# One transformer tower on one core: preparing steps, order of the maxima, place of three weight pieces, and the gates' small tiles in PSUM

## The reference, cut to what matters

```python
h = W.T[x] + b + positions                      # embedding
h = h + attn(layernorm(h))                      # 8 heads of 16, linear scores, normalised per row
y = softmax(causal(l2norm(q) * l2norm(k))) @ v @ Wo      # 2 heads of 64, on layernorm(h) twice
gate = softmax(y @ gate_W + gate_b)             # over E = 8 experts
hid  = gelu(y @ W1[e] + b1[e])                  # FF = 512 per expert
out  = sum_e gate[e] * (hid @ W2[e] + b2[e])
h = h + out
```

## Time and profile before

| | us |
|---|---|
| profiled execution, device time | 850.87 |
| its span | 849.1 |
| median of three runs | 852.5 |
| PE busy | 777.6 |
| DVE busy | 710.1 |
| ACT busy | 478.3 |
| POOL busy | 341.3 |

### The profile page before, as it was taken

The page is one execution under the profiler, slowest core; times in us unless marked ns, Lnnn a source line. Parts: engine busy times, 40 slices in busy tenths (PEclk is TensorE's granted clock), DMA queues, the critical chain, the costliest instruction groups (busy, mean ns, idle before and its releaser), DMA issues.

```text
span 849.1 us, 21002 instructions
## 1 busy us (share of the span) xinstructions
PE 777.6 (92%) x8208; PEld 555.6 (65%) x8208; DVE 710.1 (84%) x1585; ACT 478.3 (56%) x997; POOL 341.3 (40%) x386
## 2 busy tenths in 40 slices
PE   2799999999876789998889889999999999999997
PEld 1668887788644455555556556777777777777775
DVE  3668899888489776776777878999999999999997
ACT  2436555555255667776879666455555555555553
POOL 6649999777365557666667530000000000000000
PEclk9899999999799999999999999999999999999999
DMA  3101011000000000000000000000000000000000
GB/s 130 56 8 35 23 38 38 25 26 17 10 1 1 1 2 2 2 3 2 2 14 3 2 2 2 2 14 2 14 1 14 2 14 2 14 2 14 2 14 14
DMA packets 9666, 12.09 MB, mean 14 GB/s; under 512 B 1856, under 2 KB 6592, under 8 KB 9568
## 3 DMA queue, kind: packets, MB, share of 16 engines
q1 hardware_dynamic: 8544, 8.65, 3.4%
q0 software_dynamic: 1024, 2.10, 0.9%
HBM read 8.65 MB, written 2.10 MB: 13 GB/s over the span
## 4 chain that ended last, share of the span: by engine, by line
PE 75%; DVE 9%; ACT 7%; issue 5%; POOL 2%; DMA 1%; DVEq 0%; ACTq 0%; POOLq 0%
PE ps L988 73%; DVE mx L834 2%; DVE room L944 1%; ACT room L562 1%; DVE room L942 1%; ACT room L553 1%; ACT qk L492 1%; DMA h_all<-emb_rows,idx 1%; DVE mx L829 1%; PE ps L1016 1%; DVE och L911 0%; ACT qh L499 0%; PE ps L996 0%; ACT kh L501 0%; ACT hxT L481 0%
## 5 line engine op out<-in xcount | busy, mean ns | idle before, releaser
L577 ACT ACTIVATE cst<-ps,col 128x512 f32<-128x512 f32 x256 | 176.1, 689 | 164.0 <-PE ps L988 163.2
L988 PEld LDWEIGHTS ps<-arena,sq 128*128 128x128 f16 x3072 | 192.2, 98 | 62.1 <-DVE sq L972 4.2
L988 PE MATMUL ps<-arena,sq 128*128 128x128 f16 x3072 | 213.1, 219 | 0.5 <-DVE sq L972 0.5
L988 PE MATMUL ps<-y,arena 128*128 128x512 f16 x768 | 208.7, 382 | 1.3 <-DVE och L911 1.3
L972 DVE TENSOR_TENSOR sq<-cst,sq 128x512 f16<-128x512 f32 x256 | 175.8, 687 | 4.4
L373 POOL TENSOR_TENSOR room<-room 128x512 f16<-128x512 f32 (+3 forms) x122 | 123.6, 1032 | 74.2 <-ACT room L562 72.6
L967 DVE CAST sq<-cst 128x512 f16<-128x512 f32 x256 | 108.9, 425 | 11.5 <-ACT cst L577 4.2
L553 ACT ACTIVATE room<-ps 128x512 f32<-128x512 f32 (+3 forms) x160 | 76.7, 533 | 41.3 <-PE ps L988 40.9
L834 DVE TENSOR_REDUCE mx<-ps 128x2 f32<-128x1024 f32 (+2 forms) x64 | 70.1, 1096 | 30.4 <-PE ps L988 30.2
L988 PEld LDWEIGHTS ps<-y,arena 128*128 128x128 f16 x768 | 65.0, 98 | 34.0 <-issue 3.4
L960 DVE SCALAR_TENSOR_TENSOR h_all<-ps,gs,h_all 128x128 f32<-128x128 f32 x256 | 77.2, 344 | 1.0 <-PE ps L988 0.9
(11 more groups left out here) (158 smaller groups left out, 1186.9 us busy)
## 6 DMA issues: line engine op xcount, KB each, us to landing
sq<-w_rows SPq DMA_DIRECT2D x16, 256.0 KB, 2.8
out<-h_all SPq DMA_DIRECT2D x32, 64.0 KB, 1.6
cst<-consts SPq DMA_DIRECT2D x1, 896.0 KB, 5.3
h_all<-emb_rows,idx POOLq DMA_INDIRECT x32, 2.6
cst<-consts SPq DMA_DIRECT2D x1, 398.0 KB, 3.3
c<-consts SPq DMA_DIRECT2D x1, 256.0 KB, 5.1
wqkv<-w_qkv SPq DMA_DIRECT2D x1, 192.0 KB, 3.4
wsm<-w_sm SPq DMA_DIRECT2D x1, 192.0 KB, 5.1
```

Of the source, the lines that this page charges most:

```text
L577: a.activation(hid[:, f], ps[:, HBANK[f], :], ACT.Gelu_apprx_tanh, bias=col[:, K_B1 + k:K_B1 + k + 1], scale=1.0 / WS).then_inc(S["hid_rea ...
L988: return t_.matmul(o, l, r, start=start, stop=stop, skip_group_check=True)
```

## The change

The second norm from block 3 on is applied by ScalarE, with a scale and a bias that POOL and VectorE prepare; its transposition moves to the head of the preparing step. The small constant of the l2 norm is put into a 65th column of the squares, so that one addition on POOL goes. In attention the last piece of each step's pair_scores moves behind values and output parts. The three late weight pieces are treated in expert steps 2, 7 and 13, from staging tiles of their own, and the gates' biased logits and exponentials lie in bank 5 instead of in SBUF; the next user of bank 5 waits for the finished gates. In `normed_T` and `out_T` some wait counts move by one with the order.

```diff
-        eps = sb("eps", [P, 10])
-        ln_eps, l2_eps = eps[:, 0:2], eps[:, 2:10]
+        ln_eps = sb("eps", [P, 2])[:]
-        rr = sb("rr", [P, NT, 2, B])
+        rr = sb("rr", [P, NT, 4, B])
-        qk2 = sb("qk2", [P, B, 4 * DS])
+        qk2 = sb("qk2", [P, B * 4, DS + 1])
-        gt = sb("gt", [P, 2, 4, E])
+        gt = sb("gt", [P, 4, E])
+        biased = ps[:, 5, 4 * E:8 * E].rearrange("p (r e) -> p r e", e=E)
+        raised = ps[:, 5, 8 * E:12 * E].rearrange("p (r e) -> p r e", e=E)
+        late_stage = [x2_all[:].rearrange(...), hxT_all[:].rearrange(...)]
...
 SyncE
-            for n in range(2, NPIECE):
+            for n in range(2, NEARLY):
                 ...
+            sp.wait_ge(S["qkv2_ps"], NT)
+            sp.wait_ge(S["x2T_ps"], NT)
+            for n in range(NEARLY, NPIECE):
+                sp.wait_ge(S["wlow_ready"], n - 1)
+                sp.dma_start(late_stage[n % 2], w12_rows[...]).then_inc(S[STAGED[n % 2]], 16)
...
 GpSimd, both_norms
-                g.tensor_tensor(rr[:, c, 1], rr[:, c, 0], mhalf[:, 0:B], ALU.pow).then_inc(S["rr_ready"], 1)
+                g.tensor_tensor(rr[:, c, 1], rr[:, c, 0], mhalf[:, 0:B], ALU.pow).then_inc(S["neg2"], 1)
+                pool.wait_ge(S["neg2"], c + 1)
+                g.tensor_tensor(rr[:, c, 3], rr[:, c, 1], rr[:, c, 2], ALU.mult).then_inc(S["rr_ready"], 1)
 GpSimd, l2_factors
-                g.tensor_tensor(ss[:, par, 1], ss[:, par, 0], l2_eps, ALU.add).then_inc(S["l2_link"], 1)
-                pool.wait_ge(S["l2_link"], c + 1)
-                g.tensor_tensor(ss[:, par, 2], ss[:, par, 1], mhalf[:, 0:8], ALU.pow).then_inc(S["rn_ready"], 1)
+                g.tensor_tensor(ss[:, par, 1], ss[:, par, 0], mhalf[:, 0:8], ALU.pow).then_inc(S["rn_ready"], 1)
 GpSimd, end of attention
-                if s in WLATE:
-                    weights_low(NEARLY + WLATE.index(s))
+            weights_low(NEARLY)
+            weights_low(NEARLY + 1)
             low_y(LAST)
+            weights_low(NEARLY + 2)
...
 ScalarE
+            def normed2(c):
+                act.wait_ge(S["rr_ready"], c + 1)
+                act.wait_ge(S["x2T_ps"], c - 1)
+                for b in range(B):
+                    last = a.activation(x2[c % 2][:, b], h_all[:, 2 * c + b, :], ACT.Identity,
+                                        bias=rr[:, c, 3, b:b + 1], scale=rr[:, c, 1, b:b + 1])
+                last.then_inc(S["x2_ready"], 1)
             def step_b(c):
+                if c and c + 3 < NT:
+                    normed_T(c + 3)
                 if c + 2 < NT:
                     squares(c + 2)
                 high_qk(c)
                 if c == 4:
                     ao_out(NT - 1)
-                if c + 3 < NT:
-                    normed_T(c + 3)
+                if c == 0:
+                    normed_T(3)
+                if c + 4 < NT:
+                    normed2(c + 4)
+            normed2(3)
 ...
-                    a.activation(gt[:, 1], gt[:, 0], ACT.Exp).then_inc(S["eg_ready"], 1)
+                    a.activation(raised, gt[:], ACT.Exp).then_inc(S["eg_ready"], 1)
 ... (attention loop)
-                    if s in WLATE:
-                        weights_high(NEARLY + WLATE.index(s))
 ... (expert loop)
+                    if n * FT + f in WLATE:
+                        weights_high(NEARLY + WLATE.index(n * FT + f))
...
 VectorE, stats2
+                v.tensor_scalar(rr[:, c, 2], mv2[:, c, :, 0], -1.0, None, ALU.mult).then_inc(S["stats2"], 1)
 VectorE, step_b
-                if c + 3 < NT:
-                    normed2(c + 3)
 VectorE, out_part (gt[:, 0] and gt[:, 1] become)
+                    v.tensor_tensor(biased, lg, row[...], ALU.add)
+                    v.tensor_reduce(gl[:, 0], biased, AX, ALU.max)
+                    v.tensor_tensor(gt[:], biased, gl[:, 0]..., ALU.subtract)
+                    v.tensor_reduce(gl[:, 1], raised, AX, ALU.add)
+                    v.scalar_tensor_tensor(gs[:, m], raised, 1.0 / WS, gl[:, 2]..., ALU.mult, ALU.mult)
...
 TensorE, step_b
+                if c and c + 3 < NT:
+                    normed_T(c + 3)
                 if c + 2 < NT:
                     pe.wait_ge(S["qkn_ready"], c + 1)
                     project2(c + 2)
                 ...
                 unit_T(c)
-                if c + 3 < NT:
-                    normed_T(c + 3)
+                if c == 0:
+                    normed_T(3)
 TensorE, out_part 3
-                    bank5 = S["lg_ready"], m + 1
+                    bank5 = S["gate_ready"], m + 1
 TensorE, attention loop
-                for part in pairs[:1]:
+                for part in pairs[:-1]:
                     pair_scores(*part)
                 ... values(s - LAG, 0), values(s - LAG, 1) ...
-                for part in pairs[1:]:
-                    pair_scores(*part)
                 for m in range(LAST):
                     if s - YAT[m] in PE_Y:
                         out_part(m, PE_Y.index(s - YAT[m]) + 1)
+                for part in pairs[-1:]:
+                    pair_scores(*part)
 TensorE, down (experts)
+                    if NEARLY - E <= n < E:
+                        pe.wait_ge(S["wlow_ready"], E + n + 1)
-WLATE = [52, 60, 66]
+WLATE = [2, 7, 13]
```

More of the change, by code:

```diff
@@ L50, in sem @@
             return ctx.enter_context(nc.semaphore(name))
+        ps = ctx.enter_context(nc.psum_tensor("ps", [P, 8, 512], F32))
         cst = sb("cst", [P, C_END])
@@ L304, in _ @@
             g.memset(mpad[:], 0.0).then_inc(S["setup"], 1)
[L305 removed]
+            pool.wait_ge(S["setup"], 9)
             pool.wait_ge(S["load_a"], 32)
@@ L345, in _ @@
                 weights_low(n)
+            g.memset(qk2[:, :, DS:], L2_EPS).then_inc(S["eps_set"], 1)
             out_bias(NT - 1)
@@ L430, in weights_high @@
                 act.wait_ge(S[STAGED[n % 2]], 16 * (n // 2 + 1))
-                a.activation(w12[:, 4 * n:4 * n + 4, 0, :], stage[n % 2].rearrange("p (w d) -> p w d", d=D),
+                raw = stage[n % 2] if n < NEARLY else late_stage[n % 2]
+                a.activation(w12[:, 4 * n:4 * n + 4, 0, :], raw.rearrange("p (w d) -> p w d", d=D),
                              ACT.Copy, scale=WS)
-                a.activation(scaled[n % 2], stage[n % 2], ACT.Copy, scale=WS).then_inc(S["whigh_ready"], 1)
+                a.activation(scaled[n % 2], raw, ACT.Copy, scale=WS).then_inc(S["whigh_ready"], 1)
             a.preload_act_table(ACT.Exp)
@@ L491, in squares @@
                     act.wait_ge(S["wlow_ready"], NEARLY - 1)
-                a.activation(qk2[:], ps[:, q:q + B, 0:2 * D], ACT.Square).then_inc(S["sqqk"], 1)
+                a.activation(qk2[:, :, 0:DS].rearrange("p (b g) e -> p b g e", b=B),
+                             ps[:, q:q + B, 0:2 * D].rearrange("p b (g e) -> p b g e", e=DS), ACT.Square
+                             ).then_inc(S["sqqk"], 1)
                 a.copy(v16[:, 2 * c:2 * c + B, :, 0:DS],
@@ L735, in stats2 @@
                 dve.wait_ge(S["agg2"], c + 1)
-                v.tensor_scalar(rr[:, c, 0], mv2[:, c, :, 1], 1.0 + LN_EPS, LN_EPS * LN_EPS, ALU.mult, ALU.add
-                                ).then_inc(S["stats2"], 1)
+                v.tensor_scalar(rr[:, c, 0], mv2[:, c, :, 1], 1.0 + LN_EPS, LN_EPS * LN_EPS, ALU.mult, ALU.add)
+                v.tensor_scalar(rr[:, c, 2], mv2[:, c, :, 0], -1.0, None, ALU.mult).then_inc(S["stats2"], 1)
             def step_a(c, nxt, more=2, first=False):
@@ L772, in sum_squares @@
                 dve.wait_ge(S["sqqk"], c + 1)
-                v.tensor_reduce(ss[:, c % 2, 0], qk2[:].rearrange("p b (g e) -> p (b g) e", e=DS), AX, ALU.add
+                if c == 0:
+                    dve.wait_ge(S["eps_set"], 1)
+                v.tensor_reduce(ss[:, c % 2, 0], qk2[:], AX, ALU.add
                                 ).then_inc(S["ss_ready"], 1)
@@ L882, in out_part @@
                     dve.wait_ge(S["lg_ps"], m + 1)
-                    v.tensor_tensor(gt[:, 0], lg, row[:, R_GB:R_GB + E].unsqueeze(1).to_broadcast([P, 4, E]), ALU.add
+                    v.tensor_tensor(biased, lg, row[:, R_GB:R_GB + E].unsqueeze(1).to_broadcast([P, 4, E]), ALU.add
                                     ).then_inc(S["lg_link"], 1)
                     dve.wait_ge(S["lg_link"], 4 * m + 1)
-                    v.tensor_reduce(gl[:, 0], gt[:, 0], AX, ALU.max).then_inc(S["lg_link"], 1)
+                    v.tensor_reduce(gl[:, 0], biased, AX, ALU.max).then_inc(S["lg_link"], 1)
                     dve.wait_ge(S["lg_link"], 4 * m + 2)
-                    v.tensor_tensor(gt[:, 0], gt[:, 0], gl[:, 0].unsqueeze(2).to_broadcast([P, 4, E]), ALU.subtract
+                    v.tensor_tensor(gt[:], biased, gl[:, 0].unsqueeze(2).to_broadcast([P, 4, E]), ALU.subtract
                                     ).then_inc(S["lg_ready"], 1)
@@ L947, in _ @@
                     row_max(*two[1], (0, 1))
-            dve.wait_ge(S["wlow_ready"], NPIECE)
+            dve.wait_ge(S["wlow_ready"], NEARLY)
             def add_rows(n, r):
```

(14 more changed lines are left out.)

21 lines of the change are left out of this document (10 added, 11 removed).

## The result

The changed kernel takes 864.95 us (median of 4 runs, 861.81 to 865.67) against 852.18 us beside it: ratio 1.0147, 95% interval 1.011 to 1.0185. It is slower by about 12.5 us, more than the 0.5% that the prediction takes as its measure, where 853.4 and "the same" were forecast; even the upper end of the range, 859, is passed.

What follows compares the result with a forecast made beforehand. TensorE was taken as the bound, full in front and experts; preparing steps and attention could move. Terms 1.2 + 3.5 - 0.5 - 1.8 - 1.3 + 0.5 = +1.6 on 851.8 gave 853.4 us; range 850 to 857, 8 in 10 847 to 859.

Steps and rivals of the forecast that it cites:

- Front: Front: POOL's second operation in both_norms makes it later in seven gathering steps; +1.2 us, bounds 0 and 2.6.
- Preparing steps: Preparing stage: ScalarE's second norm and the earlier transposition lengthen a turn from 3.72 to 4.17 us; +3.5, bounds +1 to +5.5.
- Rival B: Preparing steps: less busy TensorE falls to its lower clock, 1.2 us more per step, five steps giving 859.5; chance 0.10.
- Order: Attention, last scores piece behind values: -5.5 of waits for maxima against costs of +2.4, +2.2, +0.4; sum -0.5 us.
- rival C: Attention: putting the maximum behind the values costs more than it gives, +5 us, 858.4; chance 0.13.
- Rival A: Attention: the new order pays in full, all but 3 us of 12.2 stalls go, -9, 844.9; chance 0.14.
- Weights: Attention: moving late weight pieces out removes a 1.20 us wait and some more; -1.8 us, bounds -3 and 0.
- Experts: Expert steps 2, 7 and 13: late weight pieces load ScalarE and slow casts beside POOL; +0.5 us, bounds 0 and 2.6.
- Gates: Attention: gates' operations on PSUM free 5.1 us of VectorE, a quarter counted; -1.3 us, bounds -5.1 and +0.5.
- rival D: Attention: the gates' hindrance on VectorE goes altogether, -5.1 instead of -1.3, 849.6 us; chance 0.08.
- Rival E: Preparing steps: ring not lengthened, ScalarE's second norm slips into its wait for project2; 849.9 us, chance 0.07.
- the forecast's upper tail: Whole kernel: the part of the forecast's spread counted as slower, beside the rivals; 0.05.

Runs made afterwards that it cites:

- e1_prep: Only the preparing steps' part (second norm on ScalarE, its multiplication on POOL, transposition first, 65th column) on the kernel before: 857.97 us, ratio 1.0089.
- e5_front: e1_prep with POOL's multiplication taken out of the front, blocks 0 to 11 sharing one after it: 859.39 us, ratio 1.0058 to the kernel before.
- e7_clock: e1_prep with four useless matmuls added in each of preparing steps 5 to 12: 860.90 us, ratio 1.0082 to the kernel before.
- e2_order: Only the new order of the maxima (last piece of scores behind values and output parts) on the kernel before: 854.77 us, ratio 1.0042.
- e9_lateorder: Kernel before with the new order of the maxima only from attention step 38 on: 850.63 us, ratio 0.9964.
- e4_gates: Only the gates' biased logits and exponentials moved to PSUM bank 5, on the kernel before: 852.89 us, ratio 1.0004.
- e6_ring: Kernel before with the transposition first in each preparing step, one block further ahead, second norm left on VectorE: 850.57 us, ratio 0.9957.
- e3_weights: Only the three late weight pieces moved from attention to the experts, on the kernel before: 849.47 us, ratio 0.9981.
- e10_best: e6_ring, e3_weights and e9_lateorder together on the kernel before: 846.68 us, ratio 0.9912.
- e11_noorder: The whole change with the old order of the maxima: 860.00 us, ratio 1.0072 to the kernel before.
- e12_bestgates: e10_best with the gates' tiles in PSUM as well: 849.83 us, ratio 0.9952 to the kernel before.
- e8_headout: e2_order with VectorE's head_out ahead of the row maxima of its step: 855.70 us, ratio 1.0027 to the kernel before.

## Why the prediction was wrong

Two steps failed most. The order's term had its gain too large and its cost too small (4.1 us, the largest miss), and the fall of the clock was put at nothing as a rival of 0.10, though it follows from the longer turn (2.8 us).

*Front* (+1.2 taken, bounds 0 and 2.6): mechanism right, size off. Seven steps by 0.375 were the upper bound, and I discounted it twice, for the 0.12 us of room and for VectorE's slack. Measured +2.2 over the thirteen powers in the traces (142.87 to 145.03 and 145.07) and 2.6 by ratios (e1_prep to e5_front, with overlapping intervals); in the profiles 1.6 of it came back before block 2's squares, at a higher granted clock, so its cost in the end isn't pinned down better than some 0.6 to 2.6. I had predicted a rise of the period by 0.1 to 0.2; it was 0.39 in the middle of the stretch. The new operation takes 0.47, longer than the L247 I had as its nearest row, and the earlier trace rows should have told me that an engine with 0.12 us of room in 11.9 is the bound already.

*Preparing steps* (+3.5, turn 4.17): right to a tenth as far as the program's order goes. The turn is 4.19, and 54.33 us were measured without the clock's fall (e7_clock) against 54.15 predicted. Inside it small sizes were off in opposite directions: the pair of activations takes 0.77 on the path, not 0.63, while the transposition and project2 behind it show 0.44 and 1.35 in the chain, together 1.79, where 0.27 and 1.54 make 1.81, and the two hand-overs of the ring are shorter.

*Rival B, chance 0.10*: came true in part, on top of the forecast rather than in place of it. That is the step that failed most in kind: a cost left out of the sum. I had listed a longer turn as certain and the clock as unlikely, though the longer turn is what makes the clock fall: in steps 0 to 4 idle matmuls stand beside the turn, after them they don't, and with such matmuls there too the fall is gone (e7_clock). Three turns at a lower clock cost 2.8 us in the trace (57.12 against 54.33), below the +3.7 from which I had it decide. The timed runs neither confirm nor refute the size.

*Order* (-0.5, bounds -7 and +4): measured +3.6, inside the bounds, at the wrong end of them. That is rival C, in its direction; its +5 on the forecast is +4.5 for the term. Both sides of the term were mis-sized. My costs were 5.0 (two pieces 2.4, head_out 2.2, step 17 0.4); items 1 to 4 lost 7.3, the low clock included. For head_out I had TensorE's wait rise by 2; it rose by 5.7 (e2_order) and 5.4 (the whole change). My gain was 5.5; free of the clock it is 2.1 in items 5 and 6, and 3.1 by e9_lateorder's time. A wait for one maximum that goes is not time gained if the moved piece's own maximum starts later by as much, and the row for that was there: each L834 takes 1.21, and a piece at a step's end with the first piece of a two-piece step behind it puts two in a row. I had priced that at 0.3 an event. Rival A is refuted.

*Weights* (-1.8): measured -1.6. *Experts* (+0.5): 0.

*Gates* (-1.3, bounds -5.1 and +0.5): measured +0.3 (-1.6 to +2.3), an interval in which -1.3 still lies. The items at equal clock give -0.3 to -0.5. L888 and L896 did fall to 0.19, some 2 us of that came back in the operations behind them (e4_gates), and of the rest hardly any was on the path. That refutes rival D's sum. The operations themselves: the Trainium skill, page "SBUF — State Buffer", section "Who interferes with whom", says that a VectorE instruction with at most one input in SBUF, outside its two-port modes, does not contend with GpSimd, and the trace agrees (0.551 and 0.462 against 0.191). The wait on gate_ready that I costed at nothing is 0.24 alone and 1.46 with the new order: "one step after VectorE's gate part" held only as long as VectorE wasn't made later by the same change.

*Rival E* (ring not lengthened): false for the whole change. e6_ring shows what it would have taken: the norm kept off ScalarE.

*The sum.* Terms measured alone: 2.2 front, 3.6 turn, 2.8 clock, 3.6 order, -1.6 weights, 0.3 gates: 10.9, of 12.5 timed (interval 9.4 to 15.8). Front, turn and clock are read from traces here; timed together they are e1_prep's 7.6, one less than the 8.6 of the three. Against mine of +1.6, the misses are order 4.1, clock 2.8, gates 1.6, front 1.0. Turn, weights and experts were within 0.5. All four misses went the same way: the costs of the front and the order were taken at a discount, the clock's was left out, and the gains of the order and the gates were taken too high. What stays open is whether the 1.6 us left are an interaction (the gs wait with the order is 1.2 of it), the low clock of three of the four runs, or the spread of the runs.

Two sums of the prediction are off without moving the verdict. The mean of the three runs and the profiled one is 851.6, not 851.8. And B, C and the forecast's upper tail make 0.28, not 0.26.

## What to carry to other kernels

Before an operation is moved to another engine, read that engine's room in a step, not its busy share, and in every stage in which the operation will run: POOL had 80% here and no room at all. If a step of a ring gets longer, price the clock with it. And where several consumers queue on one in-order engine, moving one piece later helps only where no other piece stands right behind it: split such an edit by step and time the halves, since the later steps here were worth about -3 us and the earlier ones about +7.

## What the runs showed of the hardware

TensorE's clock falls to its lower level in attention in short stretches that differ from execution to execution of like code. The item from the second to the third head_out takes 21.67 or 21.68 at full clock in seven profiled executions, those of before, e1_prep, e3_weights, e5_front, e6_ring, e7_clock and e10_best. In four others with the same order of the maxima there it is longer: 24.33 in e4_gates and e11_noorder, 23.36 in e9_lateorder and 23.46 in e12_bestgates, at PEclk 0.86 to 0.90. The lines of e4_gates and e11_noorder:

```profile
322.08:346.41 24.33, 22.41 (x301) 0.86 0.01 2
332.76:357.09 24.33, 22.41 (x301) 0.86 0.01 2
```

In e11_noorder the stretch follows a wait of TensorE of 0.78 and one of 0.50, and before had just these waits without a fall. e9_lateorder runs the program of before up to step 37, so there the fall isn't of the code. The other three are just the ones with the gates' tiles in PSUM; whether that edit favours the fall isn't settled. Item 3 takes 18.92 or 19.85 (PEclk 0.91), item 5 31.7 or 33.2 (0.95). Under the new order items 2 and 3 had it in all three profiles (e2_order, e8_headout, the whole change). So one profile of attention is uncertain by some 3 us: the profile of e6_ring has attention 3.3 us longer than before, though nothing in it was edited, while its timed ratio is 0.9957. Of these 3.3, 2.7 lie before the first head_out, behind the squares of block 15 (before, then e6_ring):

```profile
283.46:304.04 20.58, 16.07 (x195) 0.92 0.00 1
279.87:303.14 23.27, 18.80 (x195) 0.78 0.00 1
```

Lengths of single items at PEclk 1.00, and timed ratios, are what can be compared.

The stretch from the thirteenth large power to the squares of block 2 takes, in the nine profiles of kernels without an edit up to there (before, e2_order, e3_weights, e4_gates, e6_ring, e8_headout, e9_lateorder, e10_best, e12_bestgates), 25.13 at PEclk 1.00, 26.0 at 0.93, 26.94 at 0.87 and 28.5 to 28.7 at 0.82; the kernels with POOL's multiplication in the front have 26.95 to 27.16 at 0.87.

The front's start differs too: the first large power lay between 60.98 (e3_weights) and 66.61 us (e12_bestgates) in the profiles, and neither of the two has an edit in the front. It goes by the groups: 60.98 to 62.87 in e1 to e4, 63.55 to 65.11 in e5 to e8, 64.57 to 66.61 in e9 to e12, and the medians of before beside them rise in the same order, 851.37, 853.50 and 854.29 us.
